# A graph network's row gathers: Pool's writes between them given up, a smaller descriptor ring, fewer columns by TensorE

## What is computed

```python
h = relu(layernorm(x))                                   # before each layer
x = x + segment_sum(h[src] * edge_attr_32, dst) / deg + h            # layer 0
x = x + h + softmax_attention(h, src, dst, Wq, Wk, Wv) @ Wo          # layer 1
x = x + segment_sum(h[src], dst) @ W                                 # layer 2
x = x + segment_sum(tensor_product(h[src], sh0, sh1, sh2, W), dst)   # layer 3
```

## Time and profile before

| | |
|---|---|
| device time, median of 3 | 16013.85 us (15978.6 to 16015.91) |
| span of the profiled execution | 14816.7 us |
| median less that span | 1197 us |
| PE busy | 12890.3 us (87% of the span) |
| POOL busy | 12431.7 us (84%) |
| DVE busy | 9612.6 us (65%) |
| ACT busy | 3874.6 us (26%) |
| mean granted TensorE clock | 0.948 |
| gathers by Pool at L492 | 9000, 963 ns each |
| matmuls of tiles at L690 | 49406 |

### The profile page before, as it was taken

The page is one execution under the profiler, slowest core; times in us unless marked ns, Lnnn a source line. Parts: engine busy times, 40 slices in busy tenths (PEclk is TensorE's granted clock), DMA queues, the critical chain, the costliest instruction groups (busy, mean ns, idle before and its releaser), DMA issues.

```text
span 14816.7 us, 226154 instructions
## 1 busy us (share of the span) xinstructions
PE 12890.3 (87%) x57644; PEld 10677.8 (72%) x57644; DVE 9612.6 (65%) x13223; ACT 3874.6 (26%) x4265; POOL 12431.7 (84%) x18594
## 2 busy tenths in 40 slices
PE   7999999992699999999689999999769999999996
PEld 6888888881577777777578888888756666767764
DVE  7666666664577777777666666666656665666665
ACT  2222222220233333333222222222211111111111
POOL 6888888887888888888778888888888888888884
PEclk9999999995899999999889999999989999999998
DMA  5444444442344444444345555545433333333332
GB/s 174 148 148 157 157 155 151 149 151 46 101 123 122 124 124 123 122 123 124 90 119 130 129 130 128 131 127 131 110 76 87 86 90 83 90 86 87 87 86 56
DMA packets 1340717, 1727.48 MB, mean 117 GB/s; under 512 B 501932, under 2 KB 1145566, under 8 KB 1339646
## 3 DMA queue, kind: packets, MB, share of 16 engines
q10 hardware_dynamic: 705956, 1154.87, 24.6%
q1 hardware_dynamic: 327194, 407.86, 9.6%
q0 software_dynamic: 306880, 158.96, 7.6%
HBM read 1140.23 MB, written 580.36 MB: 116 GB/s over the span
## 4 chain that ended last, share of the span: by engine, by line
POOL 41%; issue 32%; PE 20%; DVE 5%; POOLq 1%; DMA 0%; DVEq 0%; ACT 0%; ACTq 0%; SPq 0%
POOL rows L492 22%; POOL pace L497 16%; PE psum L690 12%; PE psum L773 7%; POOL outs L509 2%; PE psum L764 2%; DVE work L1340 1%; DVE work L1315 1%; POOLq L496 1%; POOL q_edges L471 1%; POOL work L501 1%; DVE tile_rows L924 0%; DVE work L1323 0%; DVE rows L931 0%; DVE outs L1347 0%
## 5 line engine op out<-in xcount | busy, mean ns | idle before, releaser
L690 PE MATMUL psum<-h_parts,one_hot 128*128 128x448 f32 x49406 | 10813.2, 377 | 482.0 <-ACT one_hot L539 262.4
L690 PEld LDWEIGHTS psum<-h_parts,one_hot 128*128 128x128 f32 x49406 | 9428.8, 192 | 1500.6 <-ACT one_hot L539 313.0
L492 POOL DMA_INDIRECT rows<-h_table,idx x9000 | 8662.9, 963 | 1966.9 <-POOL pace L497 1537.1
L546 ACT ACTIVATE one_hot<-keys 128x896 fp32r<-128x896 bf16 x2533 | 2359.9, 950 | 6435.5 <-PE psum L690 4314.0
L497 POOL MEMSET pace<- 128x288 f32 x9000 | 3213.9, 357 | 18.1 <-issue 13.2
L924 DVE TENSOR_TENSOR tile_rows<-psum,h_mask 128x448 f32<-128x448 f32 x2722 | 1686.2, 619 | 1252.3 <-PE psum L690 991.3
L931 DVE TENSOR_REDUCE rows<-tile_rows 128x32 f32<-128x448 f32 x2722 | 1677.0, 616 | 58.9
L773 PE MATMUL psum<-work,bd_t 128*128 128x512 f32 (+1 forms) x3500 | 1359.2, 514 | 240.1 <-DVE work L1323 141.3
L1323 DVE TENSOR_TENSOR work<-psum,work 128x800 f32<-128x800 f32 x875 | 862.7, 988 | 920.9 <-PE psum L764 864.2
L773 PEld LDWEIGHTS psum<-work,bd_t 128*128 128x128 f32 x3500 | 654.9, 193 | 764.4 <-issue 443.4
L912 DVE TENSOR_REDUCE rows<-psum 128x32 f32<-128x448 f32 x807 | 503.1, 623 | 792.0 <-PE psum L690 741.7
(11 more groups left out here) (202 smaller groups left out, 6198.1 us busy)
## 6 DMA issues: line engine op xcount, KB each, us to landing
keys<-hots ACTq DMA_DIRECT2D x2542, 224.0 KB
keep_in<-keep_flat SPq DMA_DIRECT2D x2000, 100.0 KB
sums<-outs ACTq DMA_DIRECT2D x375, 400.0 KB
rows<-h_table,idx POOLq DMA_INDIRECT x9000
hots<-bit_hot ACTq DMA_DIRECT2D x506, 224.0 KB
hots<-work ACTq DMA_DIRECT2D x506, 224.0 KB
attn<-outs ACTq DMA_DIRECT2D x125, 800.0 KB
edge_in<-pattern_c SPq DMA_DIRECT2D x125, 400.0 KB
```

The lines of the kernel that those rows point to most:

```text
L492: nc.gpsimd.indirect_dma_start(out=rows[:, r, j * D:(j + 1) * D], out_offset=None, in_=h_table[:, :], in_offset=bass.IndirectOffsetOnAxis( ...
L546: nc.scalar.activation(one_hots[i % LOOK[l]][:, :, :], loaded_hots[i % BIT_BUFS[l]], ACT.Copy).then_inc(one_hot_cast, 1)
L690: last = nc.tensor.matmul(banks[TILE_BANKS[l][b]][:, 0:H0 * D], one_hots[hot][:, h1, :], h_parts[:, part, h1 * H0 * D:(h1 + 1) * H0 * D], ...
```

## The change

Pool's loop issues its gathers back to back, with no write, no wait and no semaphore count between them. The ring for the descriptors is 4096 bytes of a partition in place of 16384. TensorE fetches 32, 24, 32 and 20 columns per turn of five chunks in the four layers, in place of 40, 32, 40 and 28; so Pool's gathers per turn are 93, 101, 93 and 105 in place of 85, 93, 85 and 97, 9800 in all in place of 9000. The tiles in the loops go from 3500 to 2700.

```diff
-PE_COLS = ((8, 8, 8, 8, 8), (7, 7, 6, 6, 6), (8, 8, 8, 8, 8), (6, 6, 5, 5, 6))
-PACE = 288
+PE_COLS = ((7, 7, 6, 6, 6), (5, 5, 5, 5, 4), (7, 7, 6, 6, 6), (4, 4, 4, 4, 4))
+RING_BYTES = 4096
...
-        pace = sb("pace", [P, PACE])
...
-        pause_begun, pause_ended = sem("pause_begun"), sem("pause_ended")
...
-            pool.sem_inc(pause_ended, START)
...
                                 in_offset=bass.IndirectOffsetOnAxis(ap=idx[:, r, j:j + 1], axis=0)).then_inc(rows_gathered[l % 2][r], 16)
-                            pool.wait_ge(pause_ended, pauses(l, t, r, j))
-                            pool.sem_inc(pause_begun, 1)
-                            nc.gpsimd.memset(pace[:, :], 0.0).then_inc(pause_ended, 1)
...
-    nc = bacc.Bacc("TRN2", target_bir_lowering=False, num_devices=1)
+    nc = bacc.Bacc("TRN2", target_bir_lowering=False, num_devices=1, dynamic_dma_scratch_size=RING_BYTES)
```

More of the change, by code:

```diff
@@ L280, in gnn_kernel @@
         per_turn = [sum(c) for c in PE_COLS]
-        def pauses(l, t, r, j):
-            before = sum(TURNS * (RING * J - per_turn[k]) for k in range(l))
-            return t * (RING * J - per_turn[l]) + (before + sum(J - PE_COLS[l][k] for k in range(r)) + j + START)
         tile_base = [sum(TURNS * per_turn[k] + PE_COLS[k][0] for k in range(l)) for l in range(LAYERS + 1)]
```

## The result

| | before | with the change |
|---|---|---|
| device time, median of 4 each | 15996.23 us (15976.09 to 16015.91) | 20381.65 us (20360.43 to 20416.46) |
| ratio | | 1.2742, 95% interval 1.2717 to 1.2767 |
| span of the profiled execution | 14816.7 us | 20413.4 us |
| PE busy | 12890.3 us (87%) | 11870.6 us (58%) |
| POOL busy | 12431.7 us (84%) | 9888.5 us (48%) |

The change made the kernel 27% slower, where 6% faster was forecast.

The account below looks back on a forecast made before the run. Pool bounds layers 0 and 2, Pool with a chain close behind layer 1, the PE and DVE chain layer 3. Gains 213 + 150 + 213 + 433 = 1009 us from 16014 give 15005 us; own range 14,870 to 15,260, 8-in-10 range 14,450 to 15,950.

Parts of the forecast that it names:

- The pitch without writes: Pool's loops: gathers start 1.25 us apart in place of 1.47, taken from the node phase's back-to-back gathers; bounds 0.95 and 1.47.
- The second rival: Pool's loops: descriptor ring and DMA queues hold the pitch over 1.37 us; at 1.47, 17,020 us; chance 0.15.
- The ring: Descriptor ring of 4096 bytes for Pool's gathers: never fills with three in flight, costed at nothing.
- In these two layers nothing comes near Pool: Layers 0 and 2: PE (96 us per turn beside Pool's 123 in layer 0) and DVE have slack; 213 us gain each.
- The gap of 1197 us is taken as constant: Difference between profiled span and median time: unchanged by the change; if it went with the span, gain 8% larger.
- Layer 0: Pool's turn in this layer's loop falls from 131.6 to 123.1 us, over 25 turns a gain of 213 us.
- layer 2: Pool's turn in this layer's loop falls from 127.9 to 119.4 us, over 25 turns a gain of 213 us.
- 6.8 and 3.1 us per turn that are not pitch: Pool's turns in layers 0 and 2: branch back and gathers slowed by DVE's work, kept as they were.
- Layer 1: Chain DVE, PE, ACT, DVE sets the turn: 140.1 us falls to 134, bounds 129.9 and 137; gain 150 us.
- some 4 us that I had added for PE's clock after idle stretches: Layer 1's chain: PE's first tile of a chunk slower at 1.2 GHz, up to 7 us per turn; 134 us taken.
- The first rival: Chains and PE's clock take more: layer 1 gains nothing, layers 0 and 2 half; 396 us gain, 15,620 us; chance 0.12.
- Layer 3: Turn falls from 153.3 us, set by PE and DVE, to 136, with Pool closely the bound; gain 433 us.

Follow-up runs that it names:

- half-size kernels: Changed kernel with gathers of 16 of 32 values per index (13,437 and 13,412 us), or of 64 in place of 128 rows (13,183 and 13,186 us).

## Why the prediction was wrong, step by step

**The pitch without writes: right.** 1.25 us was taken from the earlier trace rows, and every unpaced kernel had it, under both conditions. The second rival, that something would hold the pitch above 1.367 us, did not happen either; it gave the right side with the wrong mechanism. It knew only one way for fast gathers to hurt, a slower Pool; that it had the side right was luck.

**The ring: right.** 15,859 and 15,925 us in one batch, with writes, and 20,107 against 20,382 us in different batches, without them and held up alike. The Trainium skill (DMA: Bandwidth & Descriptors, SWDGE vs HWDGE vs iDMA and The descriptor swizzle) had given an estimate of room for 28 gathers, where three are in flight. The runs agree in so far as the small ring cost nothing; none shows how many gathers it holds.

**"In these two layers nothing comes near Pool": the step that failed.** I costed a PE tile at 3.0 us because the earlier trace rows have it so, and let 96 us of tiles lie beside Pool's 123. The tacit assumption was that another engine's rate doesn't depend on how fast Pool issues gathers. Under the conditions of the comparison it does: layer 0 took 182 us per turn with PE busy for 62% of the window from 1000 to 3000 us. The same assumption carries the chains of layers 1 (134 forecast, 208 measured) and 3 (136 and 208). No row of the profile of before could have shown it, since it was made under good conditions and all gathers in its loops were paced.

**"The gap of 1197 us is taken as constant": the sign that I passed over.** The three timed runs lay at 15,979 to 16,016 us and the profiled span at 14,817. I had no row for it and took it as a constant. The profiles made since show 2 to 5 us between span and time (20413.4 and 20416.46 for the changed kernel). An 8% difference between two executions of one file is a finding: it says that the file has a second behaviour that the profile doesn't show. Had I taken it as such, the question would have been which of its parts is sensitive, and a kernel that deliberately slows its gathers would have been a candidate, as one possibility in the range and not as a proof.

**The terms of the sum, under the conditions of the profile.** Here the sum can be set against the run of 13,418 us. Forecast from 14,812 us: 1009 us less, 13,803. Measured: 1394 us less. The terms are read from the first and last start of the line that turns the gathered rows.
- Layer 0: forecast 213, measured 364 us; layer 2: forecast 213, measured 271 us. I had kept 6.8 and 3.1 us per turn that are not pitch; they went with the writes: 93 x 1.25 = 116.3, and in the windows 0.4 and 0.5 us remain.
- Layer 1: forecast 150, measured 3475.1 - 3247.8 = 227 us. The chain sets it, as I had it, but at 131.0 us per turn in place of 134: of the some 4 us that I had added for PE's clock after idle stretches 0.7 are left, though the granted clock did fall (0.90 in the window, 0.98 before). The first rival, with 140 us here, was wrong as well.
- Layer 3: forecast 433, measured 3743.7 - 3226.3 = 517 us. Pool is the bound there, at 131.1 us, for which I had taken 136.

These are 1379 of the 1394 us. So under these conditions the mechanism was right in all four layers and the gain too small by 28%; the recorded number is wrong because the comparison was made under the others.

**What stays open.** Three things. First, what in the chip holds the other engines up. That they want for instructions is inferred: PE's starts lie multiples of 0.7 us apart inside a tile without a semaphore, DVE and ACT stop while the work of the engines that they wait for is done, and SP issues slower. No row names it. It isn't the data queues: the gathers' packets took 5.9% of 20,413 us and 9.8% of 13,416 us, 1204 and 1315 us, so they were not slower where the engines starved, and the DMA share in the starved stretch from 3000 to 3005 us was 0.06. The rows, of the changed kernel's two pages (packets, MB, share):

```profile
q0 software_dynamic: 332480, 172.12, 5.9%
...
q14 instruction: 38, 0.31, 0.0%
```

```profile
q0 software_dynamic: 332480, 172.12, 9.8%
```

The Trainium skill (Runtime: NRT & Kernel Launch, Instruction fetch mechanics) says that each engine refills a small instruction memory by DMA in blocks of 256 instructions while it runs, which would fit engines that run on for ten us and then stop. The rows of the queues named instruction speak against it: 38 packets in the starved run, 38 in the one of 13,418 us, and 575 both in the starved kernel with tiny writes and in the unstarved one with the new columns alone; the number goes with the program. And in the starved run none of them lies between 400 and 4600 us, nearly all of layer 0's loop, in which PE was held up at 2993 us. So no refill that the trace records can be what came late there; what else supplies the engines, no row shows. Second, whether rows, descriptors or gathers count: the half-size kernels never met the poor conditions. Third, what the conditions are. One chip number showed both, the kernels of a batch seem to share them, and nothing in my hands sets them; other work on the machine at the time is not on record and not ruled out. Whether a pause longer than 288 values is faster than the kernel before under poor conditions was not measured either; under good ones it costs 1.0%.

## What to carry over

A pause that looks like waste on one engine can be what keeps the others running: before removing it, ask what its engine's rate does to engines with which it shares no semaphore, and keep the rate as a knob of its own. Treat a gap between a profiled span and the timed runs (here 14,817 and 16,014 us) as the sign of a second behaviour of the kernel and not as a constant, and run the kernel before beside every experiment, since two half-size kernels "cured" here what was simply absent in that batch. A choice such as this change is a bet on conditions: -9% under one, +27% under the other, where the pause gives up 9% under the good ones and holds the loss under the poor ones to some 10%.

## What the runs showed of the hardware that I had not expected

- While Pool issues indirect gathers of 128 rows every 1.25 us, PE, DVE and ACT can be slowed or stopped from 10 to 13 us after the burst begins for as long as it lasts; they resume 3 to 4 us after it ends. SP issues slower (6.83 us for four loads that take 1.86 otherwise). Same file: 20,382 us where this happens, 13,418 us where it doesn't.
- The effect grows steeply with the rate: at 1.43 us per gather the kernel took 17,997 us, at 1.47 us 16,234 in the same batch.
- It comes and goes on what is one chip by its number: the kernel before took 14,836 and 16,129 us there in two batches, within 0.1% among the runs of the first.
- The gap of 0.30 us behind a gather swallows a small write or a semaphore count whole: pitch 1.26, 1.25 and 1.25 us with the tiny write, with the count and with nothing.
- A descriptor ring of a quarter of the size showed no effect that one run can tell: 1.1% slower in one pair, 0.4% faster in another.
